# Layer 0 of a two-layer recurrent kernel: value products grouped behind the packs, up products moved

## The reference, cut to what matters

```python
x = L0_attn_x                                   # (8, 512, 256)
xn = _layernorm(x)
s = _L0_attn_ref(xn, ...)                       # 16 heads in 4 groups, distance bias, causal softmax
g = _silu(_L0_ffn_ref(xn, W1, W2, W3))          # silu(xn W1') * (xn W3'), Hadamard, W2
x = x + s * g
xn = _layernorm(x)
s = _L1_attn_ref(xn, ...)                       # 32 score heads (differential attention), RMS norm
g = _silu(_L1_ffn_ref(xn, ...))                 # shared expert and 8 routed experts
x = x + s * g
```

## Time and profile before

| | us |
|---|---|
| median of 3 runs | 2246.22 |
| lowest and highest run | 2242.47, 2249.08 |
| profiled execution | 2238.39 |
| its span, first to last instruction | 2236.7 |
| PE busy | 2005.8 |
| DVE busy | 1411.2 |
| ACT busy | 885.2 |
| POOL busy | 664.7 |

### The profile page before, as it was taken

One profiled execution on the slowest core, in us unless ns is written; L12 is line 12 of the kernel. 1 busy time (PEld: TensorE's weight loads), 2 busy tenths in 40 slices (PEclk: granted clock), 3 DMA queues, 4 the chain that ended last, 5 costly groups with the idle time before them and its releaser, 6 DMA issues.

```text
span 2236.7 us, 33238 instructions
## 1 busy us (share of the span) xinstructions
PE 2005.8 (90%) x11874; PEld 1438.9 (64%) x11874; DVE 1411.2 (63%) x3219; ACT 885.2 (40%) x1749; POOL 664.7 (30%) x831
## 2 busy tenths in 40 slices
PE   4299899998999899998999999999899988999898
PEld 2157667676666767576675765757666676667666
DVE  5475665666655676656757577565665666655674
ACT  2252552425433353334524245252552425433352
POOL 3341431324322242223413234131331323322331
PEclk8599999999999999999999999999999999999999
DMA  7723424243331533216332352424323153311530
GB/s 259 263 64 114 138 67 109 76 155 107 86 80 58 184 101 104 57 52 194 91 95 66 102 155 68 109 76 141 115 67 97 65 178 102 92 56 58 181 104 15
DMA packets 105380, 240.47 MB, mean 108 GB/s; under 512 B 16824, under 2 KB 27064, under 8 KB 104960
## 3 DMA queue, kind: packets, MB, share of 16 engines
q1 hardware_dynamic: 85200, 173.44, 25.9%
q0 software_dynamic: 14256, 43.94, 6.6%
q10 hardware_dynamic: 5760, 20.97, 2.8%
HBM read 179.67 MB, written 57.82 MB: 106 GB/s over the span
## 4 chain that ended last, share of the span: by engine, by line
PE 67%; DVE 8%; DMA 8%; SPq 5%; issue 4%; ACT 3%; POOL 0%; ACTq 0%; DVEq 0%
PE bank L422 21%; PE bank L584 14%; PE bank L505 11%; PE bank L471 9%; DMA qring<-mneg 8%; PE bank L521 5%; SPq L380 4%; PE bank L603 2%; DVE nmax L762 2%; PE bank L478 2%; ACT probs L662 1%; DVE bank L759 1%; ACT shared L632 1%; DVE probs L777 1%; SPq L381 1%
## 5 line engine op out<-in xcount | busy, mean ns | idle before, releaser
L422 PE MATMUL bank<-xnT,upring 128*128 128x512 f32 (+1 forms) x2208 | 708.1, 406 | 1.4 <-DVE hbuf L799 1.4
L662 ACT ACTIVATE probs<-bank 128x512 f32<-128x512 f32 (+1 forms) x752 | 407.2, 557 | 391.9 <-PE bank L505 368.5
L505 PE MATMUL bank<-qring,kring 128*128 128x512 f32 (+1 forms) x1056 | 440.6, 420 | 106.3 <-DMA qring<-mneg 63.9
L762 DVE TENSOR_REDUCE nmax<-bank 128x2 f32<-128x512 f32 (+3 forms) x544 | 354.3, 659 | 205.5 <-PE bank L478 191.1
L471 PE MATMUL bank<-kring,qring 127*128 127x512 f32 (+3 forms) x1536 | 450.3, 346 | 23.1 <-DMA kring<-k_img 11.6
L422 PEld LDWEIGHTS bank<-xnT,upring 128*128 128x128 f32 x2208 | 406.6, 193 | 59.1 <-DVE hbuf L799 9.9
L759 DVE CUSTOM_DVE_ANT_0 bank<-bank,mask_strip 128x512 f32<-128x512 f32 (+1 forms) x512 | 320.0, 635 | 164.0 <-PE bank L471 162.8
L471 PEld LDWEIGHTS bank<-kring,qring 127*128 127x128 f32 x1536 | 278.3, 196 | 108.1 <-DVE nmax L759 20.1
L505 PEld LDWEIGHTS bank<-qring,kring 128*128 128x128 f32 x1056 | 206.3, 197 | 215.5 <-DMA kring<-k_img 73.2
L584 PE MATMUL bank<-wdown,hbuf 128*128 128x256 f32 x1408 | 327.6, 382 | 0.0
L584 PEld LDWEIGHTS bank<-wdown,hbuf 128*128 128x128 f32 x1408 | 260.4, 191 | 32.5 <-issue 1.7
(11 more groups left out here) (127 smaller groups left out, 1857.8 us busy)
## 6 DMA issues: line engine op xcount, KB each, us to landing
upring<-up_img SPq DMA_DIRECT2D x136, 512.0 KB, 4.5
upring<-up_img ACTq DMA_DIRECT2D x40, 512.0 KB, 5.2
q_img<-probs SPq DMA_DIRECT2D x32, 512.0 KB, 3.7
qring<-q_img SPq DMA_DIRECT2D x256, 64.0 KB, 2.1
kring<-k_img SPq DMA_DIRECT2D x64, 256.0 KB, 3.5
qring<-q_img SPq DMA_DIRECT2D x32, 384.0 KB, 4.9
up_img<-hbuf POOLq DMA_DIRECT2D x22, 512.0 KB, 4.5
q_img<-probs SPq DMA_DIRECT2D x32, 256.0 KB, 4.6
```

Of the source, the lines that this page charges most:

```text
L422: last = nc.tensor.matmul(out_ap, part_a(a, pa, k), part_b(b, pb, k), start=(n == 0), stop=(n == len(steps) - 1))
L505: nc.tensor.matmul(SC[n % 2][:, 0:heads * w].rearrange("p (g n) -> p g n", g=heads), kring[l][:, ks, kt * P:(kt + 1) * P], qring[l][:, s, ...
L662: nc.scalar.activation(pr, pr if biased else scores, ACT.Exp, scale=scale).then_inc(s_exp, 1)
L762: nc.vector.tensor_reduce(nmax[:, u % 2, g0:g0 + heads, qt], MX[n % 2][:, 0:heads * w].rearrange("p (g n) -> p g n", g=heads), AX.X, ALU.m ...
```

## The change

The value products of all four blocks of units 0 to 2 stand in one group behind the packs, as in layer 1; in unit 3 too, behind its up products. For that, block 2 of the probabilities gets a place of its own in layer 0, `hbuf[:, 12:14]`, tiles that only layer 1 uses. The output transposes of unit u-1 move behind the turn in units 1 and 2. All up products of units 0 to 2 but the last six stand in the packs: six in unit 0 (packs 4 to 9), 18 in units 1 and 2. Of the last six, four come ahead of the turn and two behind it. On ACT the tanh of the inner tile moves from pack 6 to pack 4, and on DVE its gate half and linear half move from behind the packs to packs 5 and 9.

```diff
+UP_BEHIND = (4, 2)
...
         def third_apart(u):
 
-            return UNITS[0] <= u < U_ALL - 1
+            return u < U_ALL - 1
...
             if kt == 2 and third_apart(u):
-                return xn[0][:]
+                return xn[0][:] if layer_of(u) else hbuf[:, 12:14, :].rearrange("p a n -> p (a n)").rearrange("p (g n) -> p g n", g=G4)
...
+                    lower = u < UNITS[0]
+                    tiles = (TILE_IN[u], tile) if u in TILE_IN else (tile,)
+                    steps = [(j, half, n) for j in tiles for half in (0, 1) for n in range(UP_STEPS)]
+                    inside = len(steps) - sum(UP_BEHIND)
...
-                        if more and u in TILE_IN:
-                            pe_up_between(pe, TILE_IN[u], i)
+                        if lower and more:
+                            if u:
+                                here = range(inside * i // PACKS, inside * (i + 1) // PACKS)
+                            else:
+                                here = range(i - 4, i - 3) if 4 <= i < 4 + inside else ()
+                            for n in here:
+                                pe_up(pe, *steps[n], 1)
...
-                        if i == 3 and u not in U0 and not at_end:
+                        if i == 3 and u not in U0 and not more:
                             pe_out_turn(pe, u - 1)
-                        if i == (7, 5)[layer_of(u)] and not at_end:
+                        if u == U_ALL - 1 and i == 5:
                             pe_pv(pe, u, 0)
...
-                    if at_end:
-                        pe_up(pe, tile, 1, UP_INSIDE - UP_STEPS, 2 * UP_STEPS - UP_INSIDE)
+                    if more:
+                        if lower:
+                            pe_up(pe, tile, 1, 0, UP_BEHIND[0])
+                        else:
+                            pe_up(pe, tile, 1, UP_INSIDE - UP_STEPS, 2 * UP_STEPS - UP_INSIDE)
                         pe_max_turn(pe, u + 1)
+                        if lower:
+                            pe_up(pe, tile, 1, *UP_BEHIND)
                         if u not in U0:
                             pe_out_turn(pe, u - 1)
-                        pe_pv(pe, u, 0)
-                    if not third_apart(u):
-                        if u < UNITS[0]:
-                            pe_pv(pe, u, 1)
-                            if more:
-                                pe_max_turn(pe, u + 1)
+                    else:
+                        if lower:
                             pe_up(pe, tile, 0)
                         pe_up(pe, tile, 1)
-                    for kt in range(2 if u < UNITS[0] else 1, NT):
+                    for kt in range(1 if u == U_ALL - 1 else 0, NT):
                         pe_pv(pe, u, kt)
...
-                        if i == 6 and u in TILE_IN:
+                        if i == (4 if u < UNITS[0] - 1 else 6) and u in TILE_IN:
                             act_tanh(act, TILE_IN[u])
...
-                    if u in TILE_IN:
+                        if late and more and u in TILE_IN and i == 5:
+                            dve_gate_half(dve, TILE_IN[u])
+                        if late and more and u in TILE_IN and i == 9:
+                            dve_linear_half(dve, TILE_IN[u])
+                    if u in TILE_IN and not more:
                         dve_gate_half(dve, TILE_IN[u])
                     if late:
                         dve_bias(dve, u, PACKS - 1)
-                    if u in TILE_IN:
+                    if u in TILE_IN and not more:
                         dve_linear_half(dve, TILE_IN[u])
                         dve_normalise(dve, u - 1)
                     dve_gate_half(dve, TILE_AFTER[u])
                     dve_linear_half(dve, TILE_AFTER[u])
-                    if third_apart(u) and u not in U0:
+                    if more and u not in U0:
                         dve_normalise(dve, u - 1)
```

More of the change, by code:

```diff
@@ L1175, in unit @@
                     more = not last_of_layer(u)
-                    at_end = third_apart(u)
                     tile = TILE_AFTER[u]
+                    lower = u < UNITS[0]
+                    tiles = (TILE_IN[u], tile) if u in TILE_IN else (tile,)
+                    steps = [(j, half, n) for j in tiles for half in (0, 1) for n in range(UP_STEPS)]
+                    inside = len(steps) - sum(UP_BEHIND)
                     if more:
@@ L1190, in unit @@
                             pe_up(pe, tile, 0, i, 1)
-                        if at_end and i < UP_INSIDE:
+                        if not lower and more and i < UP_INSIDE:
                             pe_up(pe, tile, i // UP_STEPS, i % UP_STEPS, 1)
-                        if i == 3 and u not in U0 and not at_end:
+                        if i == 3 and u not in U0 and not more:
                             pe_out_turn(pe, u - 1)
-                        if i == (7, 5)[layer_of(u)] and not at_end:
+                        if u == U_ALL - 1 and i == 5:
                             pe_pv(pe, u, 0)
@@ L1326, in unit @@
                         act_exps(act, u, i)
-                        if i == 8 and third_apart(u):
+                        if i == 8 and U0[1] <= u < U_ALL - 1:
                             act_tanh(act, TILE_AFTER[u])
-                        if i == PACKS - 1 and third_apart(u):
+                        if i == PACKS - 1 and U0[1] <= u < U_ALL - 1:
                             act_max_copy(act, u + 1)
```

## The result

The changed kernel takes 2223.31 us (median of 8 runs) against 2243.02 us of the kernel before beside it: ratio 0.9922, 95% interval 0.9907 to 0.9936. Measured again on another chip it came out at 0.9926 (0.9902 to 0.9951). The profiled execution's span is 2222.1 us; before it was 2236.7. Times are compared between undisturbed executions; three on record took 3194, 3872 and 10748 us and stand outside the ratios.

The account below looks back on a forecast made before the run. PE was taken as the bound, held back in unit 0 and by ACT in unit 3. Unit 0 -2.8, units 1 and 2 -0.7, unit 3 +0.5: -3.0 us a batch, 2246.2 - 24 = 2222 us, range 2214 to 2231.

Parts of the forecast that it names:

- Unit 0, the end: Behind unit 0's turn: two up products and four blocks of value products take 2.9 us, where 3.80 us stood before.
- Unit 0, the packs: Unit 0's packs: without block 0, DVE's 2.09 us hole closes to under 0.1 us, turn 2.05 us earlier.
- the clock priced as a small term: Lower clock in unit 0's packs 6 to 8: +1.4 us where it falls, half the batches, +0.65 us on average.
- Rival one: Lower clock stays in every unit 0, as long as now; mean gain there 1.1 us; 2236 us; chance 0.2.
- the main forecast's -2.8: Unit 0 as a whole: 16.05 us against 18.83 on average, -2.8 us a batch.
- Units 1 and 2: Each unit -0.34 us, together -0.7 us a batch: turn at 675.1 instead of 674.91, 3.44 us behind it against 3.97.
- the stall that was forecast: Units 1 and 2, before the four up products ahead of the turn: PE waits 0.4 us for DVE's linear half.
- Rival three: DVE becomes the bound of units 1 and 2, each 0.85 us longer: 2241 us, no change; chance 0.09.
- Unit 3: Unit 3 gets 0.5 us longer a batch, its four blocks ending at 708.6 instead of 708.13.
- Rival four: Row of maxima becomes the wait in layer 0, as in layer 1: slower, 2268 us; chance 0.06.

Follow-up runs that it names:

- unit 3 run: Changed kernel with unit 3's value products back in their old order around its up products: 2213.47 us, ratio 0.9866 to the kernel before.

## Why the prediction was right, point by point

**The total.** 2222 us were forecast and 2223.31 measured. Part of that is luck: the forecast was -24 us from 2246.2, the median of three runs. With eight runs the kernel before has 2243.02, and the change is -17.5 us by the ratio, -19.7 by the medians and -17.3 in layer 0 of the two profiles. The sum was too large by 20 to 40%, the start 3 us too high, and the two errors cancel.

**Unit 0, the end.** Right: 2.94 us from turn to score against 2.9. The row of layer 1's unit 10 was the right one to take it from, since it held the whole sequence in one piece.

**Unit 0, the packs.** The mechanism was right: without block 0 the turn comes earlier, DVE's hole closes, and 15.4 us is what the unit takes with the clock up (15.39 in the sixth batch, the turn at 12.43 us after 12.5 forecast). The term that was too small is the clock's. The hole of 2.09 us was booked as the value products', all of it, and the clock priced as a small term on top, half the batches at 1.3 us. The kernel before with its idle time filled shows 1.5 of the 2.09 us, and 1.9 us of the unit, as the clock's own. The two added up products (2.49 of 3.87 us busy instead of 1.91) didn't keep it up: in the first profile it was down for a while in seven of eight batches, in the second in all eight. Behind the first batch such a batch takes 16.9 to 17.7 us (18.67 in one that also waits for its row), 1.5 to 2.3 over 15.4, where the sum had 1.3 to 1.4. Hence -1.95 and not -2.8 us.

How much of unit 0 runs at the lower clock differs between executions of one kernel:

| the eight units 0 | before | after | after, second profile |
|---|---|---|---|
| time at 1.2 GHz, sum, us | 46.4 | 33.3 | 48.7 |
| mean granted clock | 0.85 | 0.88 | 0.83 |
| unit 0, mean, us | 18.83 | 16.88 | 17.67 |

Rival one had the clock down in every batch and for as long as before, and 1.1 us gained. That is the second profile: 1.16 us. In the first the clock was down for 13 us less, and unit 0 gained 1.95. So the main forecast's -2.8 was met in neither, and the part of the first profile's gain that goes beyond rival one's came with a shorter spell, which no run shows to be the change's doing (the unit 3 run, whose unit 0 is the same, has 38.2 us at 1.2 GHz and 17.52 us). By the medians both measurements of the changed kernel are alike (2223.31 and 2223.77 us).

The rows could have told more: the value products at 1.84 us beside some 1.0 us were read, and DVE's hole beside them, which the same clock made, was not discounted.

**Units 1 and 2.** Right in size and steps: 16.37 us where 16.45 was forecast, 3.38 us from turn to score where 3.44 was, the stall ahead of pack 6 still 0.67 us. Timeline of PE, unit 1 of the third batch, after; it answers to the earlier trace rows:

```profile
664.04 0.44 PE L506 MATMUL bank<-qring,kring 128*128 128x384 f32 x1 [0.67 <-ACT probs L663]
...
668.71 2.06 PE L423 MATMUL bank<-xnT,upring 128*128 128x512 f32 x6
670.60 0.27 PE L485 MATMUL bank<-ident,nmax 128*16 128x128 f32 x1
...
673.98 0.50 PE L506 MATMUL bank<-qring,kring 128*128 128x512 f32 x1
```

The six products in a row (two of pack 10 and the four) take 1.9 us from the first to the turn where six in a run would take 1.5. The missing 0.4 us is about the stall that was forecast, though no row shows it as a wait: DVE is done with the previous tile's linear half at 669.51, and the first of the four products starts at 669.57. The turn is 12.99 us after the unit's start, against 12.83 before, +0.16 where +0.2 was forecast. Rival three (DVE the bound) didn't come: its two halves went into its idle times, as the rows had shown; the 1.07 us hole before the maxima of pack 8 is gone.

**Unit 3.** Right: +0.63 us against +0.5. Its wait for ACT before pack 10 grew from 0.45 us to 0.98:

```profile
697.50 0.50 PE L506 MATMUL bank<-qring,kring 128*128 128x512 f32 x1 [0.98 <-ACT hbuf L663]
697.96 3.27 PE L423 MATMUL bank<-xnT,upring 128*128 128x512 f32 x12
```

The value products had been filling such waits; the old order run showed that it is this, and not the new place of block 2.

**The row.** Rival four did not decide, but it is nearer than forecast. In unit 0 the cover is 2.94 us against the 2.44 that the row takes alone. Four rows that a load of instructions held up were late for unit 1's first score in the two profiles of the changed kernel: 3.25 and 3.42 us from turn to score in the first (row 2.5 and 2.7 us in flight), 3.07 and 3.97 in the second (2.3 and 3.2). The old cover of 3.8 us hid all but 0.07 us of such a delay (a row of 3.2 us, seventh batch of the kernel before).

**Left open.** Where the 7 us come from that the unit 3 run gained beyond its 5; the few us by which layer 1 differs between executions; and why the clock falls in one batch and not in another that does the same work.

## What to carry to other kernels

Where PE is half idle and the granted clock falls behind that, price the clock first: run the kernel with idle PE time filled by matmuls that nothing uses. Here this cost four lines and gained as much as a rearrangement of three engines; real work put at such places in the changed kernel then did the same. An idle time of another engine that was read in a stretch at the lower clock holds a share of the clock's (here 1.5 of 2.09 us): read it again with the clock up before booking it to anything else. Work moved ahead of the start of a DMA needs other work behind it as cover: each half of this change lost time or gained nothing without the other. Where PE waits for another engine anyway (unit 3), scattered pieces did better than a group. And two profiles of the changed kernel differed in unit 0 by 0.8 us of 17, mostly through the clock: compare a stage at the same granted clock.

## What the runs showed of the hardware

The granted clock fell to 1.2 GHz in unit 0 though, first batch apart, no wait of PE there was longer than 0.97 us before and 0.79 us after. The same work in the same stretch (2.49 and 2.48 us busy of 3.87) ended in a fall in one batch and not in another. With the waits filled (3.19 and 3.36 us busy of 3.87) it stayed up in all batches but the first, in four profiles. Filling shortened both the longest wait and the sum of the waits; no run tells these apart. An 8 KB row from SBUF to SBUF landed in 1.8 us with nothing else in flight; of 58 that had a load of instructions (8 or 16 KB) in flight with them 38 took more than 1.9 us, up to 3.5.
